# Gathers of the second mixture of experts into freed weight memory, with the sums on VectorE and the stores of y on the sync engine

## The reference, cut to what matters

```python
biased = xf @ centroids.T + expert_biases
_, idx = jax.lax.top_k(biased, 8)
w = sigmoid(aff taken at idx);  w = w / (sum(w) + 1e-08)
h = silu(einsum('td,edf->etf', xf, W_up))
y = einsum('etf,efd->etd', h, W_down)
routed = einsum('etd,te->td', y, cw)      # cw holds w at idx, 0 elsewhere
x = x + (shared + routed)
```

## Time and profile before

| | |
|---|---|
| median of 3 runs | 1061.76 us (1061.12 to 1062.68) |
| the profiled execution's own time | 1056.91 us |
| its span | 1055.0 us |
| PE busy | 840.2 us (80%) |
| DVE busy | 491.9 us (47%) |
| ACT busy | 383.2 us (36%) |
| POOL busy | 411.1 us (39%) |
| mean granted TensorE clock, of full speed | 0.92 |

### The profile page before, as it was taken

How to read it: one execution, slowest core, us unless ns; L and a number is a source line. 1 busy time by engine, 2 the same in 40 slices (tenths; PEclk the granted TensorE clock), 3 DMA queues, 4 the chain that set the end, 5 groups by cost and what they waited for, 6 DMA issues and landing times.

```text
span 1055.0 us, 21664 instructions
## 1 busy us (share of the span) xinstructions
PE 840.2 (80%) x6226; PEld 725.7 (69%) x6226; DVE 491.9 (47%) x1691; ACT 383.2 (36%) x1374; POOL 411.1 (39%) x401
## 2 busy tenths in 40 slices
PE   5899999899999998899998998599989998900000
PEld 4788887699999976667766666488878987800000
DVE  3666665412211236787787865265444444400002
ACT  1222222311111156565655552156556655500000
POOL 3100000111111111566666556400213078888886
PEclk9899999799999999999999999799999999955555
DMA  8466777799999839722222225577889999965556
GB/s 249 160 238 244 254 269 269 260 299 329 323 328 331 289 94 292 246 88 92 89 90 86 89 81 170 176 222 240 254 265 277 279 268 290 275 103 73 70 85 124
DMA packets 179377, 217.90 MB, mean 207 GB/s; under 512 B 13904, under 2 KB 164688, under 8 KB 179280
## 3 DMA queue, kind: packets, MB, share of 16 engines
q1 hardware_dynamic: 123408, 143.31, 42.0%
q0 software_dynamic: 25344, 44.06, 18.0%
q10 hardware_dynamic: 30528, 29.37, 8.2%
HBM read 126.64 MB, written 90.05 MB: 205 GB/s over the span
## 4 chain that ended last, share of the span: by engine, by line
PE 57%; issue 16%; DVE 10%; DMA 5%; ACT 4%; POOL 4%; POOLq 2%; DVEq 1%; SPq 1%; another core or an unknown queue 0%; ACTq 0%
PE PS L786 11%; PE PS L1034 5%; PE PS L1041 5%; PE PS L796 5%; DMA Q<-queue 4%; PE PS L654 3%; PE PS L672 3%; PE PS L865 3%; PE PS L1022 3%; PE PS L875 3%; ACT R L1238 2%; PE PS L912 2%; POOL Q L1974 2%; PE PS L632 2%; DVE nmax L1576 2%
## 5 line engine op out<-in xcount | busy, mean ns | idle before, releaser
L1974 POOL DMA_INDIRECT Q<-routed,slot x112 | 173.8, 1552 | 63.9 <-issue 32.7
L1923 POOL DMA_INDIRECT queue<-Q,slot x128 | 125.7, 982 | 86.4 <-DVE nmax L1576 53.6
L1034 PEld LDWEIGHTS PS<-Q 128*128 128x128 f32 x768 | 116.8, 195 | 24.4 <-issue 9.3
L1238 ACT ACTIVATE R<-PS,nmax 128x154 f32<-128x154 f32 x256 | 108.3, 547 | 56.5 <-DVE nmax L1576 46.1
L1034 PE MATMUL PS<-Q 128*128 128x128 f32 x768 | 120.5, 280 | 9.9 <-DVE Q L1763 5.2
L786 PEld LDWEIGHTS PS<-R 128*128 128x128 f32 x992 | 115.2, 192 | 4.3 <-issue 2.6
L786 PE MATMUL PS<-R 128*128 128x128 f32 x992 | 116.2, 275 | 1.3 <-ACT R L1200 1.1
L1763 DVE COPY Q<-R 128x256 f32 x192 | 58.2, 304 | 126.1 <-PE PS L1041 86.4
L1041 PE MATMUL PS<-R,Q 128*128 x384 | 116.3, 386 | 0.0
L1307 ACT ACTIVATE Q<-PS 128x128 f32<-128x128 f32 x192 | 53.5, 279 | 99.9 <-PE PS L1041 77.7
L1022 PE MATMUL PS<-ident,Q 128*128 128x128 f32 x384 | 76.9, 283 | 9.8 <-DMA Q<-queue 9.1
(11 more groups left out here) (281 smaller groups left out, 1588.3 us busy)
## 6 DMA issues: line engine op xcount, KB each, us to landing
R<-in_gate_up SPq DMA_DIRECT2D x31, 1024.0 KB
Q<-queue SPq DMA_DIRECT2D x192, 160.0 KB
routed<-pads SPq DMA_DIRECT2D x16, 1536.0 KB, 6.9
routed<-Q ACTq DMA_DIRECT2D x96, 256.0 KB
R<-in_down SPq DMA_DIRECT2D x31, 512.0 KB
queue<-pads SPq DMA_DIRECT2D x16, 640.0 KB, 3.3
R<-in_W_up SPq DMA_DIRECT2D x16, 512.0 KB
R<-in_W_down SPq DMA_DIRECT2D x8, 1024.0 KB
```

The lines of the kernel that those rows point to most:

```text
L1034: pe.matmul(up1_bank(j), w_now[:, j % BEHIND, c, :], x1T[:, j % BEHIND, c, :], start=(c == 0), stop=(c == KC - 1))
L1238: i = act.activation(prob[:, g % 2].rearrange("p (k h) -> p h k", h=HG)[:, h, :], src, ACT.Exp, bias=nmax2[:, g % 2, h:h + 1], accum_out=d ...
L1923: pool.indirect_dma_start(out=queue1, out_offset=bass.IndirectOffsetOnAxis(ap=slot1[:, t * TOP1 + k:t * TOP1 + k + 1], axis=0), in_=pay[:, ...
L1974: pool.indirect_dma_start(out=acc[:, t, :], out_offset=None, in_=routed1, in_offset=rows, compute_op=ALU.add).then_inc(S(f"acc_in{t}"), 16)
```

## The change

Three things change. ACT no longer issues the stores of y; SP does, at odd i from 15 on, right after `load1(i)`. The gathers no longer add: rank r of token tile t is written to a place of its own, which for ranks 0 to 6 is the memory of the weights of expert 8 r + t / 2 (up weights for even t, down weights for odd t), and for rank 7 (`IN_R`) the tile `acc`. DVE adds the ranks after the loop: 12 additions of 128x2048 (each rank from 1 to 6, even and odd t), then 16 operations that scale the sum and add it to X, then 16 that do the same with rank 7. Because a gather now overwrites weights, its need is the larger of the row's pair and the pair in which the expert whose memory it takes has its last tile (`own_expert`, `end_col`, `need_row`), and the tiles that are left over use expert 63's weights and not expert 0's. The rank now lies outermost in `slot1` and `need1`.

```diff
+        def sum_part(r, odd):
+            at = odd * NUP + r * (NT // 2) * D
+            return R[:, at:at + NT // 2 * D]
+        def gathered(r, t):
+            return acc[:, t, :] if r == IN_R else sum_part(r, t % 2)[:, t // 2 * D:(t // 2 + 1) * D]
 # sync engine
+            def store1(m):
+                k = m % (RING // PAIR)
+                for i in range(PAIR):
+                    sp.wait_ge(S(f"y1_{i}"), nth(f"y1_{i}", m + 1))
+                rows = routed1[m * PAIR * P:(m + 1) * PAIR * P, :].rearrange("(n p) d -> p n d", p=P)
+                sp.dma_start(rows, y1[:, PAIR * k:PAIR * (k + 1)]).then_inc(S(f"y1_out{k}"), 16)
...
                     load1(i, at[i % RING])
+                if i % PAIR == 1 and 0 <= i - LAG < NX1:
+                    store1((i - LAG) // PAIR)
                 if i % PAIR == 1 and i >= LAG + LAND:
                     land1((i - LAG - LAND) // PAIR)
 # scalar engine
-                if j - BEHIND >= 2 and (j - BEHIND) % 2 == 0:
-                    store1((j - BEHIND) // 2 - 1)
-            store1(NX1 // PAIR - 1)
 # tensor engine, in begins()
+                pe.wait_ge(S("end_rows"), nth("end_rows", 1))
+                pe.matmul(bank(2)[0:1, 3 * P:4 * P], end_col[0:E1, :], own_expert[0:E1, :], start=True, stop=True).then_inc(S("end_row_ps"), 1)
 # vector engine
+                dve.tensor_tensor(need_row[0:1, :], need_row[0:1, :], bank(2)[0:1, 3 * P:4 * P], ALU.max).then_inc(S("need_max1"), 1)
...
+            def sum_rank(r, odd):
+                for t in range(odd, NT, 2):
+                    dve.wait_ge(S(f"acc_in{t}"), nth(f"acc_in{t}", 16 * (r + 1)))
+                if r > 1:
+                    dve.wait_ge(S("summed"), 2 * (r - 2) + odd + 1)
+                dve.tensor_tensor(sum_part(0, odd), sum_part(0, odd), sum_part(r, odd), ALU.add).then_inc(S("summed"), 1)
+            for r in range(1, IN_R):
+                for odd in range(2):
+                    sum_rank(r, odd)
             for t in range(NT):
+                dve.wait_ge(S("summed"), 2 * (IN_R - 2) + t % 2 + 1)
+                dve.scalar_tensor_tensor(X[:, t, :], gathered(0, t), rstd_all[:, t:t + 1], X[:, t, :], ALU.mult, ALU.add).then_inc(S("most"), 1)
+            for t in range(NT):
+                dve.wait_ge(S("most"), t + 1)
                 dve.wait_ge(S(f"acc_in{t}"), nth(f"acc_in{t}", 16 * TOP1))
-                dve.scalar_tensor_tensor(X[:, t, :], acc[:, t, :], rstd_all[:, t:t + 1], X[:, t, :], ALU.mult, ALU.add).then_inc(S("final"), 1)
+                dve.scalar_tensor_tensor(X[:, t, :], gathered(IN_R, t), rstd_all[:, t:t + 1], X[:, t, :], ALU.mult, ALU.add).then_inc(S("final"), 1)
 # gpsimd
-            for k in reversed(range(TOP1)):
+            for r in range(TOP1):
                 for t in range(NT):
-                    i = t * TOP1 + k
+                    i = r * NT + t
                     need = pool.value_load(need1[0:1, i:i + 1], min_val=1, max_val=NX1 // PAIR)
                     pool.wait_ge(S("landed"), need)
                     pool.sem_inc(S("waited_pool"), 1)
-                        pool.wait_ge(S(f"acc_in{t}"), nth(f"acc_in{t}", 16 * (TOP1 - 1 - k)))
-                        pool.indirect_dma_start(out=acc[:, t, :], out_offset=None, in_=routed1, in_offset=rows,
-                                                compute_op=ALU.add).then_inc(S(f"acc_in{t}"), 16)
+                    if r:
+                        pool.wait_ge(S(f"acc_in{t}"), nth(f"acc_in{t}", 16 * r))
+                    pool.indirect_dma_start(out=gathered(r, t), out_offset=None, in_=routed1,
+                                            in_offset=bass.IndirectOffsetOnAxis(ap=slot1[:, i:i + 1], axis=0)).then_inc(S(f"acc_in{t}"), 16)
```

More of the change, by code:

```diff
@@ L67, in build @@
     LAG = 14
+    IN_R = TOP1 - 1
+    BIG = float(1 << 15)
     LAND = 4
@@ L313, in build @@
         x1T, w_now, h1T = q(BEHIND, KC, P), q(BEHIND, KC, F1), q(4, P)
-        tile_rows = q(NT, TOP1)
+        tile_rows = q(TOP1, NT)
         acc = q(NT, D)
-        active1, began1, row_at, ones1, begin_diag = (acc[:, i, 0:n] for i, n in enumerate((NX1, NX1, NX1, P, E1)))
+        active1, began1, row_at, ones1, begin_diag, own_expert, end_col, need_row = (acc[:, i, 0:n] for i, n in enumerate((NX1, NX1, NX1, P, E1, P, 1, P)))
         PS = ctx.enter_context(nc.psum_tensor("PS", [P, 8, BANK], F32))
@@ L1315, in out_x1 @@
                 act.activation(y1[:, k], down1_bank(j), ACT.Copy, scale=w_col[:, j % AHEAD:j % AHEAD + 1]).then_inc(S("y1_0"), 1)
[L1317 to L1322, removed]
             for j in range(BEHIND):
@@ L1742, in _ @@
             dve.tensor_scalar(row_of[:, :], row_at[0:1, :], 0.0, None, ALU.max).then_inc(S("row_of1"), 1)
-            dve.tensor_copy(expert_of[:, :], bank(2)[0:1, 0:NX1]).then_inc(S("expert_of1"), 1)
+            dve.tensor_scalar(expert_of[:, :], bank(2)[0:1, 0:NX1], float(E1 - 1), None, ALU.add).then_inc(S("expert_of1"), 1)
             step("expert_of1")
@@ L1782, in begins @@
                 dve.memset(ones1, 1.0).then_inc(S("ones1"), 1)
-                dve.tensor_scalar(begin_col[:, :], first, float(P), None, ALU.add).then_inc(S("begin_col"), 1)
+                dve.tensor_scalar(begin_col[:, :], first, float(P) + BIG, None, ALU.add).then_inc(S("begin_col"), 1)
                 step("begin_col")
                 dve.tensor_scalar(begin_diag[0:E1, :], ident[0:E1, 0:E1], begin_col[:, :], None, ALU.mult).then_inc(S("begin_diag"), 1)
+                dve.memset(own_expert, 0.0).then_inc(S("own_zero"), 1)
+                step("own_zero")
+                mine = IN_R * NT // 2
+                dve.tensor_copy(own_expert[0:E1, 0:2 * mine].rearrange("p (e i) -> p e i", i=2),
+                                ident[0:E1, 0:mine].unsqueeze(2).broadcast_to([E1, mine, 2])).then_inc(S("own_expert"), 1)
+                dve.tensor_tensor(end_col[0:E1, :], start, ntiles, ALU.add).then_inc(S("end_col"), 1)
+                step("end_col")
+                dve.tensor_scalar(end_col[0:E1, :], end_col[0:E1, :], float(P), None, ALU.mult).then_inc(S("end_rows"), 1)
             def moved(t):
-                dve.tensor_tensor(row(weight, t), row(weight, t), bank(2)[:, 0:E1], ALU.subtract).then_inc(S("moved1"), 1)
+                dve.tensor_tensor(row(weight, t), bank(2)[:, 0:E1], row(weight, t), ALU.subtract).then_inc(S("moved1"), 1)
                 dve.wait_ge(S("moved1"), nth("moved1", t + 1))
@@ L1791, in moved @@
                 dve.wait_ge(S("moved_sel1"), nth("moved_sel1", t + 1))
[L1792 removed]
+                dve.max(tile_rows[:, :, t], row(weight, t)).then_inc(S("best_rows1"), 1)
             def rows():
                 dve.wait_ge(S("best_rows1"), nth("best_rows1", NT))
[L1796 removed]
+                dve.tensor_scalar(slot1[:, :], tile_rows.rearrange("p r t -> p (r t)"), -1.0, BIG - 1.0, ALU.mult, ALU.add).then_inc(S("rows1"), 1)
             def last():
                 step("lastT_ps")
[L1800 removed]
+                dve.tensor_reduce(last_row[:, :], bank(2)[:, P:2 * P], X_AXIS, ALU.min).then_inc(S("last1"), 1)
             def needs():
                 step("need_ps")
[L1804 removed]
+                dve.tensor_scalar(need_row[0:1, :], bank(2)[0:1, 2 * P:3 * P], -1.0, BIG, ALU.mult, ALU.add).then_inc(S("need_row1"), 1)
+                step("need_row1")
+                dve.tensor_tensor(need_row[0:1, :], need_row[0:1, :], bank(2)[0:1, 3 * P:4 * P], ALU.max).then_inc(S("need_max1"), 1)
+                step("need_max1")
+                dve.tensor_scalar(need1[:, :], need_row[0:1, :], float(PAIR * P - 1), None, ALU.add).then_inc(S("need_up1"), 1)
                 step("need_up1")
```

14 lines of the change are left out of this document (5 added, 9 removed).

## The result

The changed kernel takes **1071.52 us** (median of 20 runs, 1063.92 to 1078.9), the one before 1059.64 us beside it (20 runs, 1054.68 to 1065.58). The ratio is 1.0116 with a 95% interval of 1.0094 to 1.0137: slower, where 1006.5 us had been forecast. The profiled execution took 1074.62 us, its span is 1072.8, its mean granted clock 0.903.

The account below looks back on a forecast made before the run. POOL's list of gathers was taken to set the end from 846.45 us on. Span: 1055.0 - 55.8 (shorter gathers) + 0.6 (needs) = 999.8 us; carried over to the runs, 1061.76 - 55.2 = 1006.5 us, range 992 to 1030.

Parts of the forecast that it names:

- the loop's end: Expert loop: taken to end at 924.3 us as before; a slower loop after 846.45 us was said to cost little.
- The gathers, 0.95 us: POOL: all 128 gathers become plain ones of about 0.95 us instead of 1.55, with the gap staying 0.30 us.
- 1.43 us within the loop: POOL's interval between gathers inside the expert loop, set by its sequencer's slow register reads; 1.257 us behind the loop.
- the first rival: POOL's gathers keep 1.257 us within the loop as well; time 997 us, chance 0.16.
- The additions, 2.33 us: DVE: twelve 128x2048 additions of 2.33 us, 28 us together, costing nothing, with 1.7 us to spare.
- the second rival: DVE's additions stop POOL's reads or descriptors, adding 28 us to POOL's list; time 1034 us, chance 0.12.
- The stores on SP cost nothing: Stores of y issued by SP: nothing taken for the loop up to 846.45 us; bounds 3 us less, 14 us more.
- I expect no wait there: SP's stores: y was written some steps earlier by DVE and ACT, so SP should not wait for it.
- The third rival: Late-landing stores on SP slow the loop: mild, 1021 us, chance 0.07; slower than the kernel before, chance 0.05.
- The needs, 0.6 us: Six small DVE operations and one PE matmul put 0.6 us on the path, bounds 0 and 3; later gather release, nothing.

Follow-up runs that it names:

- a1: The changed kernel with the stores of y back on ACT; 1079.47 us, ratio 1.0119.
- a2: The kernel before with only the stores of y moved to SP, its gathers still adding; 1067.71 us, ratio 1.0017.
- d1: The kernel before with the addition taken out of its gathers, so seven ranks are left out of the sum; 1047.81 us, one run.
- d3: The changed kernel without the register reads ahead of gathers, waiting for one constant per rank instead; 1112.69 us, one run.
- a3: The changed kernel with all gathers held until all stores have landed, so none runs within the loop; 1113.17 us, one run.
- a4: The changed kernel with a small POOL operation (0.56 us) ahead of all 128 gathers; 1087.22 us, ratio 1.0198.
- b1: The changed kernel with a 0.56 us POOL operation ahead of each of the first 60 gathers; 1043.33 us, ratio 0.98.
- b3: The changed kernel with a 0.56 us POOL operation ahead of every fourth of the first 72 gathers; 1073.65 us, ratio 1.0052.
- b2: The changed kernel with a 0.56 us POOL operation ahead of every second of the first 66 gathers; 1033.87 us, ratio 0.9695.
- c3: c1 with the stores of y back on ACT; 1024.58 us, ratio 0.9622.
- c5: c3 with the pacing of every second gather carried on to the end of the list; 1028.74 us, ratio 0.9708.
- c1: b2 with the running sum of the ranks kept in PSUM, where ACT copies the first rank; 1028.08 us, ratio 0.9647.

## Why the prediction was wrong

**The step that failed is the loop's end.** The working took 924.3 us over from the trace of before and argued only how much later it might come without harm ("After 846.45 a slower loop costs little", with over 20 us for DVE to spare). It came 105 us later. Behind it stands DVE's chain, 12 additions, 32 operations and the store, 43.5 us as measured from loop end to end of span. The forecast had 999.8 - 924.3 = 75.5 us there, so the chain was covered for 32 us. The other 105 - 32 = 73 us are the whole difference between the span forecast, 999.8, and that measured, 1072.8. The cause is in none of the rivals. a1 and a2 take the stores out of question, d1 the destination, the needs and DVE's sums, d3 the register reads, a3 shows that the loop alone is whole, and a4 and b1 to b3 that it is how closely plain gathers follow each other. So the saving of 0.6 us per gather, on which the forecast rested, itself brought the closeness that stopped the other engines. The trace of before held the warning: its one "remote" wait stands behind its one close series of plain gathers. I took from that series the gap between gathers and not what the other engines did beside it.

**The gathers, 0.95 us**: right. All 128 are plain, with a median of 954 ns, and the gap is 0.30.

**1.43 us within the loop**: wrong in its reason. Reads are short (median 293 ns, against 527 in the loop before), and where nothing stalls the interval is 1.26, as the first rival had it. With the stalls and the landing waits the mean from 852.55 to 1018.72 is 1.54, so the list ended 27 us later than the 991.7 forecast, and was still not the end.

**The additions, 2.33 us**: right in size (2.28; 26.5 us for twelve) and wrong as "cost nothing". With the loop late they are on the path to the end in full.

**They hold POOL up** (the second rival, 0.12): the mechanism is real. Gathers take 2.2 to 2.4 us in a3 and a4 beside additions, and 15.6 us of gather time go when one operand and the result move to PSUM. The price was named too high: 28 us, where b2's gathers take 19 us more than 128 of 954 ns. In the changed kernel it costs nothing, as no gather is left when the additions start. The earlier trace rows had no operation as long as these beside a gather, and its silence was read as evidence. Nor did it have a series: the operations of line 1836 came one at a time, with 1.25 us and more between them, and a3 shows what such short ones do without a gap, a gather of 5.23 us.

**The stores on SP cost nothing**: right for the time (1.0017), and SP's wait for landings fell instead of rising. "I expect no wait there", for y, was nearly right: 6.4 us in 15 waits. Answering to the earlier trace rows, from 640 to 1000 us:

```profile
SPq L469 <- DVE w_col L1769: 56.2, 52, 8.0
SPq L477 <- ACT Q L1336: 6.4, 15, 1.0
SPq L482 <- DMA routed<-Q: 0.2, 1, 0.2
```

The third rival, the only one that ended above before, falls as the mechanism: its long waits for landings aren't there, and its slow loop came from elsewhere. Whether the stores on SP slow the loop by a few us more stays open. Among the kernels without stalls the last matmul starts at 920.8 (c3) and 916.2 (c5) with them on ACT, and at 919.8 to 927.8 (b1, a4, b2, c1) with them on SP; a2 has 938.0.

**The needs, 0.6 us**: no run isolates them. The 20th gather was released at 852.55 and not at 846.45; three of the 19, 10.8 us of ACT's waiting, lie before 850 (one of 3.9 in the kernel before) and can explain it, so nothing is left over that would have to be theirs.

**What stays open.** What exactly a dense list of plain gathers blocks isn't shown. The trace shows that the release by a matmul, finished by the profile's modelled end, reaches ACT and DVE late and together, and that POOL's sequencer stretches at the same time. Whether a mean interval between 1.41 and 1.57 us is the border or the number of gathers between two breaks isn't separated; eight with a mean of 1.47 us made one stall in the kernel before. Whether adding gathers would do the same at that density can't be tried, as they take 1.55 us each. In the windows from 850 us on PE's granted clock is 0.54 to 0.74 in place of 1.00, and PE is idle for a quarter to a half of the time; the clock's own share in the loss wasn't separated.

## What to carry to other kernels

A shorter descriptor job on POOL is not free for the others: when gathers follow each other more densely than they did, look at whether PE, ACT and DVE stand at the same moments, and try a small pause between gathers (here one of 0.56 us ahead of every second one turned a ratio of 1.0116 into 0.9695) before giving the idea up. A tail that is to be hidden needs its cover computed from a loop end that the change itself may move. For sums that run beside gathers it is worth trying to keep the running sum in PSUM; here that took 15.6 us off the gathers.

## What the runs showed of the hardware that was not expected

- Plain gathers of 128 rows at 1.26 us stop PE, ACT and DVE together, mostly for 4 to 8 us (changed kernel), and for up to 21.8 us in a series without register reads (d3); with pairs of gathers at a mean of 1.57 us none of it appears (b2). In the kernel before eight of them were enough for one stall of 3.9 us. The share of the DMA engines is then only 0.5 to 0.7.
- A gather that adds takes 1.55 us of POOL, one that doesn't 0.95. The slower kind kept the kernel before clear of the stalls: d1, which differs in nothing else, has 15.
- POOL's register read takes 0.29 us behind the loop of before and 0.53 in the median within it. Beside plain gathers in the loop its median is 0.29 to 0.30 in the changed kernel, b2 and c3 (from 846 us on), but 0.35 in b1 and 0.40 in a4. What sets it isn't shown.
- A 128x2048 float32 addition takes 2.28 us whether its first operand and result lie on chip with the second (2282 ns) or in PSUM (2293 ns). The gathers into R beside the former reach 2.63 us (b2), those beside the latter 1.09 (c1). Operations of 0.47 us each that read two operands on chip do the same when they follow each other without a gap (5.23 us in a3).
